# Two-layer transformer on one Trainium2 core: second attention with the token stream's buffer kept, operands loaded ahead, and the softmax denominators applied in the output projection

## What is computed

```python
q = (hidden_states @ q_w.T).reshape(b, s, NH, HD).transpose(0, 2, 1, 3)
...
scores = jnp.einsum('bhqd,bhkd->bhqk', q, kf) / jnp.sqrt(jnp.asarray(HD, dt))
scores = jnp.where(causal, scores, jnp.finfo(dt).min)
attn = jax.nn.softmax(scores, axis=-1)
out = jnp.einsum('bhqk,bhkd->bhqd', attn, v)
out = out.transpose(0, 2, 1, 3).reshape(b, s, NH * HD)
return out @ o_w.T
```

## Time and profile before

| | us |
|---|---|
| median of 3 runs | 2313.44 |
| lowest, highest | 2312.14, 2317.91 |
| the profiled execution | 2313.69 |
| its span, first to last instruction | 2311.9 |

### The profile page before, as it was taken

How to read it: one execution, slowest core, us unless ns; L and a number is a source line. 1 busy time by engine, 2 the same in 40 slices (tenths; PEclk the granted TensorE clock), 3 DMA queues, 4 the chain that set the end, 5 groups by cost and what they waited for, 6 DMA issues and landing times. The chain is left out here.

```text
span 2311.9 us, 54178 instructions
## 1 busy us (share of the span) xinstructions
PE 2077.5 (90%) x22192; PEld 1468.3 (64%) x22192; DVE 1544.6 (67%) x2534; ACT 874.0 (38%) x1836; POOL 486.2 (21%) x408
## 2 busy tenths in 40 slices
PE   7999969999988999778888888888888699999997
PEld 5777758877766788634444444444444588787776
DVE  6544423799966354478989988889998330477776
ACT  4222123222213200045655655565665221234443
POOL 0111112222310145401111111111111444221111
PEclk9999989999998999979999999999999899999999
DMA  5122154344326533333443333343332555320101
GB/s 179 56 93 75 38 195 151 109 134 132 121 94 250 177 121 121 110 77 84 102 106 99 93 100 87 84 113 107 92 92 77 214 170 183 111 90 19 55 1 37
DMA packets 197121, 251.26 MB, mean 109 GB/s; under 512 B 38496, under 2 KB 119712, under 8 KB 194208
## 3 DMA queue, kind: packets, MB, share of 16 engines
q1 hardware_dynamic: 196032, 247.85, 34.7%
q10 hardware_dynamic: 864, 0.21, 0.0%
HBM read 165.08 MB, written 82.90 MB: 107 GB/s over the span
## 5 line engine op out<-in xcount | busy, mean ns | idle before, releaser
L1614 ACT ACTIVATE a_prob<-ps,a_nmax 128x256 f32<-128x256 f32 (+7 forms) x512 | 377.4, 739 | 349.4 <-DVE a_nmax L1642 211.2
L1727 PE MATMUL ps<-a_kt,a_q 64*128 64x512 f32 (+5 forms) x1536 | 380.4, 536 | 85.3 <-ACT a_prob L1614 63.6
L1642 DVE TENSOR_REDUCE a_nmax<-ps 128x1 f32<-128x1024 f32 (+3 forms) x256 | 256.1, 1000 | 73.0 <-PE ps L1727 71.5
L1659 DVE STREAM_TRANSPOSE a_pt_long<-a_prob 128x512 f32<-128x512 f32 (+3 forms) x512 | 278.1, 580 | 0.0
L1727 PEld LDWEIGHTS ps<-a_kt,a_q 64*128 64x128 f32 x1536 | 143.1, 193 | 184.5 <-ACT a_prob L1614 116.7
L1741 PE MATMUL ps<-a_pt_long,a_v 32*64 32x256 f32 (+3 forms) x7808 | 228.6, 344 | 2.5 <-issue 1.0
L2021 DVE SCALAR_TENSOR_TENSOR f_part<-ps,f_gu_scale,f_part 128x512 f32<-128x512 f32 x264 | 184.6, 745 | 65.8 <-PE ps L2068 52.5
L1741 PEld LDWEIGHTS ps<-a_pt_long,a_v 32*64 32x64 f32 x7808 | 153.9, 132 | 105.1 <-issue 77.1
L1694 POOL TENSOR_TENSOR a_o<-a_left 128x256 f32<-128x256 f32 x128 | 90.3, 726 | 595.5 <-ACT a_left L1624 595.5
L940 POOL TENSOR_TENSOR f_hT_lo<-f_h,f_hT_hi 128x512 fp32r<-128x512 f32 x64 | 89.7, 1407 | 294.5 <-ACT f_hT_hi L923 294.5
L1724 PE MATMUL ps<-a_causal,a_identb 64*128 64x128 bf16 x1024 | 112.2, 224 | 39.5 <-ACT a_prob L1614 39.5
(11 more groups left out here) (228 smaller groups left out, 4552.4 us busy)
## 6 DMA issues: line engine op xcount, KB each, us to landing
a_q<-scratch_QT SPq DMA_DIRECT2D x512, 64.0 KB, 2.1
scratch_QT<-k_qo SPq DMA_DIRECT2D x64, 256.0 KB, 2.3
a_v<-scratch_V SPq DMA_DIRECT2D x64, 256.0 KB, 4.3
scratch_OT<-a_o SPq DMA_DIRECT2D x32, 512.0 KB, 3.4
o_of<-scratch_OT SPq DMA_DIRECT2D x32, 512.0 KB, 4.1
f_block<-in_packed SPq DMA_DIRECT2D x33, 256.0 KB, 3.4
f_mask<-scratch_maskT SPq DMA_DIRECT2D x16, 512.0 KB, 5.1
a_kt<-scratch_KT SPq DMA_DIRECT2D x128, 64.0 KB, 4.2
```

The source lines that it names most:

```text
L1614: last = nc.scalar.activation(prob[:, n % PRING, s].rearrange("p (a w) -> p a w", w=w), SC[n % 2][:, a, 0:w], ACT.Exp, bias=nmax[:, n % 4, ...
L1642: nc.vector.tensor_reduce(nmax[:, n % 4, 0:1], SC[n % 2][:, :, 0:width(0, t)], AX.XY, ALU.max, negate=True).then_inc(maxed, 1)
L1659: last = nc.vector.transpose(pt[hf][:, lo:hi, h, t - FIRST[hf], :], src.rearrange("p (j k) -> p j k", k=32))
L1727: last = pe.matmul(sc[:, a, 0:w], q[r, slot, heads[a * hf], :], kt[r, b, keys], start=not masked, stop=True, skip_group_check=True)
```

## The change

- `feed_forward0`: the second product runs block by block over all four token tiles, and waits for each block by itself.
- `projections1`: two small tables come first and are all that ScalarE and TensorE wait for; then all weights; then the four large tables. Between the last stores SP loads the attention's first operands (three query tiles, keys, values, masks) into `xacc`, whose content is in x2 by then. The block no longer waits for the last query stores; the attention's SP does.
- `attention1` keeps keys, values, queries and masks in `xacc`. The ring of query tiles has 3 places instead of 4, the probabilities 4 instead of 8. Transposed long probabilities have two buffers (`pt_long` for blocks 0 to 23, `pt_wide` for the rest); no transpose is cut by time. Short values stand at steps 26 to 30, long values at 34 to 46. Spreading, denominators by matmul, and scaling on GpSimd are gone: values are evicted unscaled (two instructions a half), one reciprocal a unit is transposed and stored to a new scratch tensor R. After the last score, SP loads the output projection's first operands into `xacc`.
- `output1`: VectorE multiplies each row block by the inverse denominators, loaded from R with a broadcast over 64 partitions; step 0 runs in two pieces.

The diff, cut:

```diff
-                        for bs in (range(BPQ - 2), range(BPQ - 2, BPQ)):
-                            pe.wait_ge(h_lo.sem, h_lo.now(it, bs[-1] + 1))
+                        for b in range(BPQ):
+                            pe.wait_ge(h_lo.sem, h_lo.now(it, b + 1))
                             for t in range(TPC):
-                                if bs[0] == 0:
+                                if b == 0:
                                     pe.wait_ge(y_added.sem, y_added.before(it, t + 1))
-                                for b in bs:
-                                    last = split_matmul(pe, YB[t], hT, [w[:, p] for w in w2], b == 0, b == BPQ - 1,
-                                                        np.s_[:, b, t * P:(t + 1) * P], np.s_[:, b, :])
-                                if bs[0] > 0:
+                                last = split_matmul(pe, YB[t], hT, [w[:, p] for w in w2], b == 0, b == BPQ - 1,
+                                                    np.s_[:, b, t * P:(t + 1) * P], np.s_[:, b, :])
+                                if b == BPQ - 1:
...
+        CONSTS = [(cosk[:], d["c_cosk"]), (sink[:], d["c_sink"]), (cosq[:], d["c_cosq"]), (sinq[:], d["c_sinq"])]
...
+                sp.dma_start(eps[:], d["c_eps"]).then_inc(first_in.sem, 16)
+                sp.dma_start(ident[:], d["c_ident"]).then_inc(first_in.sem, 16)
+                for n, name in enumerate(names):
...
+                q, kt, v, identb, causal = attention1_rooms(xacc)
+                sp.wait_ge(x2_stored.sem, 16)
+                for s in q_stored:
+                    sp.wait_ge(s.sem, s.now(1, 0))
+                for k in range(QRING):
+                    tok = slice((ST - 1 - k) * P, (ST - k) * P)
+                    for a in range(2):
+                        for j in range(2):
+                            r = a * HD1 + j * HD1 // 2
+                            sp.dma_start(q[r:r + HD1 // 2, k, :, :],
+                                         d["QT"][0, j, :, tok].rearrange("(h p) t -> p h t", h=HQ)
+                                         ).then_inc(ahead.sem, 16)
+                store_q(NKV - 1, 0)
                 sp.wait_ge(k_stored.sem, k_stored.now(NCH, 0))
+                for a in range(2):
+                    for part in range(4):
+                        r = a * HD1 + part * 16
+                        sp.dma_start(kt[r:r + 16, 0, :], d["KT"][part, 0:16, 0:SEQ]).then_inc(ahead.sem, 16)
+                store_q(NKV - 1, 1)
                 for s in v_stored:
                     sp.wait_ge(s.sem, s.now(NCH, 0))
-                for s in q_stored:
-                    sp.wait_ge(s.sem, s.now(NKV, 0))
+                for i in range(4):
+                    sp.dma_start(v[32 * i:32 * i + 32, 0, :, :], d["V"][0, 0, :, :, :]).then_inc(ahead.sem, 16)
+                for dst, src in ((identb, d["c_identb"]), (causal, d["c_causal"])):
+                    for a in range(2):
+                        sp.dma_start(dst[a * HD1:(a + 1) * HD1, :, :], src.rearrange("(s p) k -> p s k", s=2)
+                                     ).then_inc(ahead.sem, 16)
+                for c in range(2, NCH):
+                    store_q(NKV - 1, c)
+                sp.wait_ge(x_stored.sem, 32 * NCH)
+                sp.wait_ge(ahead.sem, 16 * (4 * QRING + 8 + 4 + 4))
...
-                act.wait_ge(c_in.sem, ALL_CONSTS)
+                act.wait_ge(first_in.sem, 32)
...
-QRING = 4
-PRING = 8
+QRING = 3
+PRING = 4
 FIRST = (4, 0)
 BLOCKS = (32, 16)
-
-FRONT, BACK, WHOLE = range(3)
-TURNS = {i + 2: [(i, FRONT)] for i in range(LONG)}
-for r, back in {5: (0,), 6: (1,), 7: (2, 3), 8: (4,), 9: (5, 6), 10: (7, 8)}.items():
-    TURNS[r] += [(i, BACK) for i in back]
-for i in range(9, LONG):
-    TURNS[i + 2] += [(i, BACK)]
-TURNS.update({i + 2: [(i, WHOLE)] for i in range(LONG, USTEPS)})
-MIDDLE = 16
-
-LONG_VALUES = {18 + i: range(3 * i, 3 * i + 3) for i in range(10)}
-LONG_VALUES[28] = range(30, 32)
-SHORT_VALUES = {31 + i: range(2 * i, 2 * i + 2) for i in range(8)}
-LONG_LEFT = {28: (0, 1), 29: (2, 3)}
-SHORT_LEFT = {38: (0, 1), 39: (2, 3)}
-LONG_STORE, SHORT_STORE = 34, 44
-LATEST = 45
+MAIN = 24
+LATER = 2
+
+SHORT_VALUES = {26: range(0, 3), 27: range(3, 6), 28: range(6, 9), 29: range(9, 13), 30: range(13, 16)}
+LONG_VALUES = {34: range(0, 2), 35: range(2, 4), 36: range(4, 6), 37: range(6, 8), 38: range(8, 10), 39: range(10, 11),
+               40: range(11, 13), 41: range(13, 15), 42: range(15, 18), 43: range(18, 21), 44: range(21, 24),
+               45: range(24, 28), 46: range(28, 32)}
+SHORT_LEFT = {31: (0,), 32: (1,)}
+LONG_LEFT = {47: (0, 1)}
+SHORT_STORE, LONG_STORE = 34, 50
+INVERT = USTEPS + 2
+LATEST = 53
...
+                        src = prob[:, n % PRING, i * blocks * 32:(i + 1) * blocks * 32]
+                        src = src.rearrange("p (j k) -> p j k", k=32)
+                        if hf:
+                            last = nc.vector.transpose(pt_short[:, 0:blocks, h, t, :], src)
+                        else:
+                            near = min(blocks, MAIN)
+                            last = nc.vector.transpose(pt_long[:, unit % 2, 0:near, h, t - 4, :], src[:, 0:near, :])
+                            if blocks > MAIN:
+                                last = nc.vector.transpose(pt_wide[:, unit % 2, 0:blocks - MAIN, h, t - 6, :],
+                                                           src[:, MAIN:blocks, :])
...
+                def invert(u):
+                    dve.wait_ge(exped, (u + 1) * USTEPS)
+                    nc.vector.reciprocal(rden[:], den[:, u % 2, :]).then_inc(inverted, 1)
+                    dve.wait_ge(inverted, u + 1)
+                    wait(dve, r_stored, 64 * u)
+                    nc.vector.transpose(rdenT[:], rden[:]).then_inc(r_turned, 1)
...
+                        nc.scalar.activation(
+                            o[:, i % 2, :, :, 2 * k:2 * k + 2, :].rearrange("p s t i q -> p i (s t) q"),
+                            PV_ALL[:, 2 * k:2 * k + 2, 0:256].rearrange("p i (w q) -> p i w q", q=32), ACT.Copy
+                            ).then_inc(evicted, 1)
...
+                stage, of, rd = output1_rooms(xacc)
+                for k in range(2):
+                    sp.dma_start(stage[:, k, :], d["WoG"][0, :, k, :]).then_inc(ahead, 16)
+                    sp.wait_ge(o_stored[k], 16)
+                sp.dma_start(of, d["OT"][0, :, 0:SEQ]).then_inc(ahead, 16)
+                sp.wait_ge(r_stored, 64)
+                for a in range(2):
+                    sp.dma_start(rd[a * HD1:(a + 1) * HD1, :], d["R"][0, 0, a, :].partition_broadcast(HD1)
+                                 ).then_inc(ahead, 16)
...
+                        if n:
+                            dve.wait_ge(o_in[n % 3], 48 * (n // 3 + (1 if n % 3 else 0)))
+                        nc.vector.tensor_tensor(row(n, s), row(n, s), inverse(n, s), ALU.mult).then_inc(scaled, 1)
```

304 lines of the change are left out of this document (147 added, 157 removed).

## The result

| | before | after |
|---|---|---|
| median of four runs, us | 2312.79 | 2276.68 |
| range of the runs, us | 2311.39 to 2317.91 | 2270.9 to 2280.8 |
| span of the profiled run, us | 2311.9 | 2271.8 |

The ratio of after to before is 0.9834, with a 95% interval of 0.9813 to 0.9856: a gain of 36 us by the medians and of 33 to 43 by the interval, where 73 were forecast. The forecast of 2240 us is 37 us too low, and 2276.68 lies 6 us above the range of 2220 to 2271.

A forecast was written before the change was run, and what follows sets the result against it. In the second attention neither TensorE nor VectorE is full; each step costs the larger of the two. The terms sum to -73.6 us: 2311.9 becomes 2238.3, with the 1.8 around it 2240 us; range 2220 to 2271.

The forecast's parts named there:

- Term 10: Output projection: with the added multiplications a round takes 5.3 us against TensorE's 5.44 and just fits; +0.5 us (0 to +5).
- Term 4: Attention units: nearly every unit has a clock dip after steps 7 to 9, at 0.7 to 1.3 us; +6 us (0 to +15).
- Rival E: Attention units: half clock stays after sparse steps 7 to 9, some 8 us more a unit; whole 2360 us; chance 0.04.
- Term 5: Attention tail: both value parts of the last unit follow the last score, 23 us instead of 17; +6 us.
- Term 1: Attention order and buffers: values and transposes placed better, a unit 46.4 instead of 49.93 us, 15 units; -53 us.
- Rival A: Attention: long transposes (640 and 768 columns) are dearer than the slope, +15 us; whole 2255 us; chance 0.10.
- rival B: Attention: score, maximum and exponential, or late query tiles, keep the unit at 49.9; only joints won, 2287 us; chance 0.08.
- Term 3: Attention's unit 0: 48 us instead of 52.1, half clock returning while values are missing; -4 us (0 to -8).
- Term 6: Projections to attention: first operands loaded between the last stores, so the first score comes at 973.3; -14.3 us.
- rival D: End of the projections: loads hold up the stores, 5.5 us; whole 2246 us; chance 0.06.
- Term 7: Start of the projections: ScalarE waits for two small transfers instead of four tables; -7.5 us (-5.5 to -8.5).
- Term 8: First feed-forward: TensorE's wait for GpSimd's low half goes, VectorE's 22.9 us period stays; -2.5 us once (0 to -8).

The follow-up runs named there:

- e1: Changed kernel, but the output projection loads the inverse denominators only for steps 1 and 2 and multiplies later rows by those; 2255.3 us, ratio 0.9750.
- e4: Changed kernel with normalisation moved back into the attention (GpSimd multiplies, VectorE for the last unit), no factor loads or multiplication in the output projection; 2255.2 us, ratio 0.9726.
- e2: Changed kernel with the output projection's factor loads replaced by same-size loads in which each partition reads a row of its own; 2273.9 us, ratio 0.9823.
- e3: Changed kernel, all loads kept, but output projection rows after the first are not multiplied; 2269.8 us, ratio 0.9809.
- e5: Changed kernel with 8 filler matmuls in each of steps 7, 8 and 9 of every attention unit; 2264.9 us, ratio 0.9765.
- e10: Changed kernel with normalisation in the attention, the other table of values, and fillers in steps 7 and 8, first unit, tail and before output projection; 2226.8 us, ratio 0.9620.
- e11: Changed kernel with the start of the second projections as before (four tables loaded between second and third weight and waited for); 2277.6 us, ratio 0.9840.
- e8: Changed kernel with the first feed-forward as before (blocks 0 and 1 awaited together); 2281.3 us, ratio 0.9850.
- e6: Changed kernel with another table of values: short values in steps 3 to 6, evictions a step earlier, long values from step 9; 2248.0 us, ratio 0.9715.

## Why the prediction was wrong

The direction and most steps were right; the sum failed at three terms.

**Term 10, the multiplications in the output projection: +0.5 us forecast (0 to +5), +14.1 measured.** The step costed three engines, 5.3 us a round against 5.44 of TensorE, and left out the fourth resource: the DMA. Each step got 512 KB of factors beside 512 KB of its row, and the rest of the stage (weights, 4 MB of token stream, some 8 MB ahead for the next stage) was there already. The loads of the factors stand in no term at all. The trace of before would have warned, but not given the size: the kernel before moved 30.8 MB in this stage, 174 GB/s, with the DMA engines busy for 50%; the change adds 16 MB, half as much again, which at the same price per byte makes 76%. That it came to 90% of a longer stage, and to 98.5% from 1780 to 1940, is because the transfers get dearer as they meet (o_of lands after 5.2 us instead of 4.1), and that no row of before shows. e1 and e4 take the bytes away and get 178.8 and 177.8; e2 and e3 show that neither the broadcast nor the multiplication matters.

**Term 4, the clock in the units: +5.6 us for fourteen units forecast, +15.7 measured** (14.4 of them with half clock, 1.3 the open unit 5). The mechanism was named with its place, steps 7 to 9, and its upper bound (+15) nearly held. Mis-sized was the price of one dip: 0.7 to 1.3 us, taken from dips of before that lasted 3.4 us. After, most last 6.8 us and cost 2.55 (49.05 less 46.50), and those of 3.4 us cost 1.6 (48.07 less 46.50). The number of dips was too high: nearly every unit was to have one, seven of fourteen had, and this hid part of the error in the price. The dips of before lie elsewhere, too. The prediction put all four behind steps 15 to 17. Those of units 8 and 15 are there; the one of unit 3 falls in steps 13 and 14, and the one of unit 10 at the same place. In that of unit 3 VectorE stays busy nearly all the time, which is why it cost only 0.67 us (unit 8 lost 1.43):

```profile
1167.20:1170.60 3.40, 3.40 (x40) 1.60 (x38) 3.12 (x6) 1.77 (x4) 0.00 (x0) 0.50 0.08 25
```

The dips of after run on into steps 10 and 11, where TensorE at half clock is the later one. Rival E, the same mechanism at 8 us a unit, did not come; of the Trainium skill's section ("TensorE: Matmul & The Clock Gate", "HAM oscillation — how this bites in real kernels"), by which a pause in each round brings the low clock back in each round, the trace shows a fall in seven of fourteen units, and e5 shows the cause.

**Term 5, the tail: +6 us forecast, and 7 more measured.** The parts were right at full clock: 22.8 us in e10 against 23. The clock was left out: the prediction asked what sparse steps do to it inside the units and not what the two pauses of the tail do, before the short values (for the last exponentials and transposes) and before the long ones (for the eviction). Short values then ran at 0.66 and long ones at 0.84 of the clock. The last unit and its tail held 20.5 us of half clock against 4.4 before. One dip of 6.8 us is unit 15's own, so that up to 2.5 of the 7 us belong to term 4.

Term 1 was right: 46.50 us for an undisturbed unit against 46.4, 3.43 against 3.5 gained. The method, adding up both queues step by step and taking the larger in each, is good to 0.1 us here. Rival A is out with the transposes, and rival B, whose 2287 us was nearer to the measured time than the forecast, is out with the unit of 46.50: the total alone would have misled. Term 3, unit 0: -3.7 against -4. Term 6: the first score 0.54 us after the last store's issue, -13.7 against -14.3; rival D (5.5 us) is out, 0.7 is the most that the stores lost. Term 7: -7.0 against -7.5, and e11 takes it back to the hundredth. Term 8: -4.0 against -2.5, e8 gives 4.1; inside its bounds (0 to -8); it is the 4.0 us by which TensorE's waits for the low half shrank, where the prediction had let TensorE get ahead once by 2.5. Term 9: -4.6 against -4.8. Term 2: no wait of TensorE for a query tile is in the trace.

Of the signs that the prediction named, units of 46 to 47 us and both engines above 90% were seen only without dips (41.8 and 44.1 of 46.5, 90% and 95%); dips after the steps without values were seen; units of 48 us or more, named as a sign of being wrong, were seen seven times; a tail of 23 us was not (31 behind an undisturbed unit, some 28 behind one with a dip), and TensorE waiting for o_oT_lo in the output projection, named as a sign of being wrong, was (6.9 us between 1780 and 1940). The range missed because it added bounds of single terms, each from its own rows, and no term had the DMA's bytes in it.

## What to carry to other kernels

- Beside the engines a stage has a budget of bytes: before a transfer is moved into one, add up all that the stage moves and compare with the DMA share in the same window, with room left for transfers that get dearer as they meet. The same loads cost 14 us in a stage of 177 us where the DMA engines stood at 50%, and nothing spread over the attention's 790 us, where they stood at 36%.
- A table that lets two engines take turns had better not leave TensorE with several light steps in a row: move values into them (e6, 27 us in 15 units), and where that can't be done, add a few matmuls that nobody reads (e5, 16 us). These are worth it only where the step has idle time to spare (e10: nothing gained).
- Where a gain of some us must be seen among executions that differ by 10, compare the stage in the trace, not the median.

## What the runs showed of the hardware that was not expected

- A load that writes 64 partitions from one row of 4 KB is as dear as one of 64 rows: 191.3 and 191.9 us for the stage, 98.5% and 98.2% of the DMA engines. At that share they moved 272 and 268 GB/s.
- 6.8 us of half clock cost a unit 2.55 us in the changed kernel, 3.4 us cost 1.6 there and 0.93 in e6: less than or about the half that TensorE loses. In the windows above VectorE is the later engine for part of such a dip.
- With matmuls that nobody reads in steps 7 to 9, no dip of the clock began in any of units 1 to 14, where seven of them had one without (e5).
- GpSimd multiplying 128 x 512 elements out of SBUF (1.27 us) left VectorE's transposes as they were (961 against 962 ns, e4), while GpSimd's subtraction lengthened VectorE's multiplication of two SBUF operands by about the time that they overlapped, from 1.21 to as much as 3.47 us (e1).
